# Left-over queries in plain fp32, row places and kept norms on GpSimd, and the weighting of the values spread over two slots of an attention pipeline

## The chip, the cores and the metric

The program runs on one core of one Trainium2 chip. The metric is the device time of one execution in microseconds. TensorE is called PE in the profile (PEld is its weight load), VectorE DVE, ScalarE ACT, GpSimd POOL and the DMA-issuing SyncE SP.

## The reference, cut to what matters

Each of 32 images is cut into 196 patches, projected to 128 features, joined with 77 text tokens to N = 273 tokens, and sent through attention with mixed heads and then through a mixture of 8 experts with two chosen per token. All is fp32.

```python
h = concatenate([tok(x), txt], axis=1)                  # 32 x 273 x 128
qkv = layernorm(h) @ w_qkv.T + b_qkv                    # 8 heads of 16
q, k = rope2d(q), rope2d(k)
logits = einsum('bhid,bhjd->bhij', q, k) * d ** -0.5
logits = einsum('bhij,gh->bgij', logits, w_pre)         # heads mixed before ...
attn = softmax(logits)
attn = einsum('bhij,gh->bgij', attn, w_post)            # ... and after the softmax
h = h + einsum('bhij,bhjd->bhid', attn, v) @ w_out.T + b_out
y = layernorm(h)
top_p, top_i = top_k(softmax(layer_norm(y, ln_g, ln_b) @ Wg), 2)     # two experts per token
h = h + layer_norm(y + combined, out_g, out_b)          # combined: two experts' outputs by their shares
```

## The kernel before, in words

**The two halves.** A first stage runs over the images (32 steps and two more to drain) and does tokens, attention, and the routing of each image's rows into a DRAM table `routed`. A second stage runs the experts over 76 tiles of 256 routed rows, and a third adds the results up. The change is in the first stage, but for two waits behind it.

**The first stage.** The head mix `w_pre` is folded into the queries (a head's query is the whole 128-feature query times a column of factors), and the mix `w_post` into the values (`VP`, one copy of the values for each head). So a head's scores are one product of 128 features with 273 keys. 273 queries are two tiles of 128 (`MQ` = 256) and `RT` = 17 left-over ones; the left-over queries of all 8 heads are packed into two tiles of 68 rows. One step `i` is thus 9 slots `u` (`NU`): slot 0 scores the left-over queries (`qrf`, split into `qrh` and `qrl`), slots 1 to 8 one head each. Each engine has an order of its own, written out by hand in its `step(i, par, has)`, and they meet only in semaphores. `par` is the parity of the step, which chooses between double buffers. The step is a software pipeline over four images: in step `i` image `i` is in attention, image `i + 1` is embedded (`emb`), image `i - 1` gets its residual (`res`), image `i - 2` is routed (`rout`), and the rows of image `i - 3` are scattered (`late`). Steps 4 to 29 are a hardware loop of two steps a turn, the others are written out.

**Per slot.** PE multiplies scores (`scores`, L1258, into two PSUM banks), transposes the probabilities of three slots earlier (`probs_T`), and multiplies those of four slots earlier with `VP` (`weighted`). DVE takes the sums' reciprocals and scales half of the probabilities of the slot before (`row_sums`, `head_probs`), takes the row maxima (`head_max`), and makes the low part of a query tile (`q_lo`). ACT copies the transposed probabilities to SBUF (`probsT`, L709), scales the other half (`scaled`), makes the high part of a query tile (`q_hi`) and takes the exponentials (`exps`, L682). POOL scales the left-over queries' part (`rest_keys`, L503). A scores product of fp32 precision is three fp32r products: high by high, high by low, low by high.

**What stands where around the change.** Slot 1 and 2 of PE: `x2T_` (L1335, the transposes of image `i - 2`, which need `xhat` of ACT, L762), then `tok` (L1225, 12 matmuls each, the tokens of image `i + 1`), which write the PSUM bank `MA` that the values of image `i` lie in, and so wait until `values` of DVE (L916 twice, and L922 into `VR`) has read them. `values` is called in DVE's slot 0. Slot 8 of PE: `rank` (the places of the rows within each expert, L1354 to L1358) and then `vproj` (L1255, the values of image `i + 1`, into `MA`). Slot 8 of DVE: `k_lo` (L939), `qr_lo` (L934), `q_lo`, and `places` (L1020 to L1032): position of each row from `rank` and the running `base`, times the two choice masks `mk`, summed over the 8 experts, cast to integers `slu`. POOL's `scatter` (L564, six indirect DMAs) uses `slu` in slots 0 and 1 of the next step. POOL's slot 5 has `norm2` (L513 to L525, powers on 98x3), its slot 6 `rope_add` of the queries (L486, `qT`) and `rest_queries` (L494, `qrf`), its slot 7 `rope_add` of the keys (`kT`) and the routing masks. ACT has `qr_hi` (L666) in slot 7 and `k_hi` (L745) in slot 8. DVE's `keep` (L982) copies the norms of image `i - 2` into `kept`, read at the end of the program. After the last image DVE makes the tile table from `base` (L1113 to L1140) and SP writes the tails and loads tiles.

Of the kernel before, what the change touches and what calls it, by code (L numbers as in the profile page):

```python
# [25 lines left out]
B, C, IMG, P16 = 32, 3, 224, 16  # L26
HP = IMG // P16
TXT, D, NH, DH = 77, 128, 8, 16
NE, FH = 8, 512
# [3 lines left out]
NT = 3  # L33
# [51 lines left out]
def early_fusion_kernel(nc, x, txt, w_tok, w_qkvr, small_in, w1, b2, w2, rope, tail, tiota,  # L85
# [5 lines left out]
    with ctx:  # L91
# [22 lines left out]
        rounded_ = sb("rounded", [D, 4 * NP + 8 * MQ + 2 * NH * RT], f32r)  # L114
# [41 lines left out]
        at += 2 * QR * MQ  # L156
        qrh, qrl = (rounded_[:, at + i * NH * RT:at + (i + 1) * NH * RT] for i in range(2))
# [44 lines left out]
        slf = sb("slf", [R, 2, NT])  # L202
# [25 lines left out]
        def parts(buf, count, size, at=0):  # L228
# [21 lines left out]
            k_hi k_lo q_hi q_lo qr qr_hi qr_lo vp scores_ps max exp recip probs probs_act own probsT_ps probsT_sb av_ps attn_sb proj_ps h1  # L250
            rstd2 rstd2_steps y2 xhat x2T_ps x2T_sb gate_ps gate_sb top8 logit_gap gap_exp choice_steps masks both
            share_steps routed_cols rank_ps pos_steps pos_read slots scat0 scat1 table_steps table_ready ends_ready
# [175 lines left out]
        def _(pool):  # L428
# [45 lines left out]
            def rope_add(b, par, n):  # L474
# [6 lines left out]
                else:  # L481
                    if not below(b, 1):
                        pool.wait_ge(S["k_hi"], b)
                        pool.wait_ge(S["k_lo"], b)
                    dst = kT[:]
                g_.tensor_tensor(dst, rc[:, n, :], rsn[:, n, :], ALU.add).then_inc(S["qk_sb"], 1)  # L486

            def rest_queries(b, par):

                pool.wait_ge(S["qk_sb"], 2 * b + 1)  # L490
                if not below(b, 1):
                    pool.wait_ge(S["qr_hi"], b)
                    pool.wait_ge(S["qr_lo"], b)
# [12 lines left out]
            def norm2(b):  # L506
# [18 lines left out]
                g_.tensor_tensor(rr2[:], tv2[:, 0], mhalf[:], ALU.pow).then_inc(st, 1)  # L525

# [28 lines left out]

            def scatter(j, par, k):
# [45 lines left out]
            steps(pool, step)  # L602
            scatter(B - 1, 1, 0)
# [37 lines left out]
        def _(act):  # L641
# [19 lines left out]

            def qr_hi(b):
                act.wait_ge(S["qr"], b + 1)
                if not below(b, 1):
                    act.wait_ge(S["scores_ps"], NU * (b - 1) + 1)
                nc.scalar.copy(qrh[:], qrf[:].rearrange("p g n -> p (g n)")).then_inc(S["qr_hi"], 1)  # L666
# [100 lines left out]
            qr_hi(0)  # L767
# [3 lines left out]
            def step(i, par, has):  # L771
                for u in range(NU):
# [26 lines left out]
                    if u == 7 and has["emb"]:  # L799
                        qr_hi(i + 1)  # L800
# [48 lines left out]
        def _(dve):  # L849
# [82 lines left out]
            def qr_lo(b):  # L932
                dve.wait_ge(S["qr_hi"], b + 1)
                v.tensor_tensor(qrl[:], qrf[:].rearrange("p g n -> p (g n)"), qrh[:].bitcast(f32), ALU.subtract  # L934
                                ).then_inc(S["qr_lo"], 1)

# [42 lines left out]
            def keep(j):  # L979

                dve.wait_ge(S["rstd2"], j + 1)
                v.tensor_copy(kept[:, bass.ds(j, 1)].rearrange("p a n t -> p (a n) t"), nr2[:])  # L982

# [18 lines left out]
            def experts(j):  # L1002
# [12 lines left out]
            def places(j, par):  # L1015

                st = S["pos_steps"]
# [535 lines left out]
```

## Time and profile before

| | us |
|---|---|
| Three runs | 1542.67, 1545.71, 1545.99 (median 1545.71) |
| The profiled execution, its own time | 1548.41 |
| Its span in the trace | 1546.6 |
| Busy: PE, PEld, DVE, ACT, POOL | 1213.4, 1094.2, 1102.9, 1049.4, 885.5 |
| Image step, from the starts of the 32 copies of L731 | 32.8 |

The profiled execution has 1.8 us around its span, and stands 0.17% above the median. The first image step's slots begin at about 29 us, the last attention step ends near 1083 us, and experts and sums fill the rest. All busy shares are averages over these stages. The granted PE clock is 0.931 over the whole span and 1.00 in the steps quoted below.

### The profile page before, as it was taken

To read this page: it belongs to the slowest core of one execution; us is meant where nothing else is said; L and a number is where in the kernel's file an instruction comes from. 1 tells how busy PE (TensorE), PEld (TensorE's weight loads), DVE (VectorE), ACT (ScalarE), POOL (GpSimd) and SP (SyncE) were. 2 spreads that over 40 slices of the span, in tenths; PEclk is the share of its full clock that TensorE was granted. 3 is DMA by queue.
4 is the path that set the end of the run, shared out by engine and by line. 5 is a ranking of instruction groups with operands and counts; after the bars stand their busy time and mean duration, and the time that the engine had idled before them with its cause. 6 is when DMAs were issued, how large, how long until landed. Compare 5 with 4: busy or idle time off the path is not lost.

```text
span 1546.6 us, 36424 instructions
## 1 busy us (share of the span) xinstructions
PE 1213.4 (78%) x8770; PEld 1094.2 (71%) x8771; DVE 1102.9 (71%) x3668; ACT 1049.4 (68%) x3071; POOL 885.5 (57%) x1653
## 2 busy tenths in 40 slices
PE   5898888888888888888888888888459999996000
PEld 4777777777777777777777777777359999996000
DVE  4877887788877888877888878886145445443887
ACT  2688777777777877777777777777035555553665
POOL 2136555556555556554565555565436666675998
PEclk8999999999999999999999999999579999998555
DMA  5001110010111010110010110100032222222454
GB/s 219 18 26 30 47 37 30 29 33 29 46 34 32 29 33 29 47 35 30 29 33 29 49 34 29 33 14 16 18 88 78 79 74 76 77 75 65 140 156 133
DMA packets 69517, 82.80 MB, mean 54 GB/s; under 512 B 11626, under 2 KB 59725, under 8 KB 68898
## 3 DMA queue, kind: packets, MB, share of 16 engines
q1 hardware_dynamic: 57216, 57.16, 12.6%
q0 software_dynamic: 11328, 19.07, 4.1%
q10 hardware_dynamic: 866, 5.55, 0.9%
q14 instruction: 89, 0.73, 0.2%
q8 instruction: 18, 0.29, 0.1%
HBM read 52.08 MB, written 30.65 MB: 53 GB/s over the span
## 4 chain that ended last, share of the span: by engine, by line
PE 40%; DVE 25%; issue 15%; POOL 8%; ACT 7%; DVEq 2%; DMA 1%; SPq 1%; ACTq 0%; POOLq 0%
PE PS L1464 9%; PE PS L1225 6%; PE PS L1311 4%; DVE rounded L929 4%; DVE nmax L965 4%; ACT E L682 3%; PE PS L1451 2%; PE PS L1452 2%; PE PS L1453 2%; DVE VP L916 2%; PE PS L1248 2%; DVE bst L871 2%; DVE sl L1024 2%; POOL rs L634 2%; DVE xn L896 2%
## 5 line engine op out<-in xcount | busy, mean ns | idle before, releaser
L1311 PE MATMUL PS<-AT,VP 128*128 128x273 f32 x1024 | 281.3, 397 | 0.0
L682 ACT ACTIVATE E<-PS,nmax 128x273 f32<-128x273 f32 x512 | 243.6, 482 | 36.5 <-DVE nmax L965 36.3
L965 DVE TENSOR_REDUCE nmax<-PS 128x2 f32<-128x546 f32 (+1 forms) x288 | 205.9, 715 | 73.5 <-PE PS L1273 73.5
L564 POOL DMA_INDIRECT dram_routed<-xr,slu x192 | 203.7, 1061 | 64.5 <-issue 64.5
L1271 PE MATMUL PS<-rounded 128*128 128x274 f32 (+1 forms) x576 | 209.1, 363 | 5.0 <-DVE rounded L934 3.1
L615 POOL DMA_INDIRECT dram_results<-arena,du x152 | 166.1, 1093 | 64.2 <-issue 54.6
L1311 PEld LDWEIGHTS PS<-AT,VP 128*128 128x128 f32 x1024 | 177.0, 193 | 21.0
L1291 PE MATMUL PS<-small,E 128*128 128x128 f32 x1024 | 157.6, 276 | 39.8 <-ACT ATR L716 39.8
L1272 PE MATMUL PS<-rounded 128*128 128x274 f32 (+1 forms) x576 | 169.4, 294 | 0.0
L1273 PE MATMUL PS<-rounded 128*128 128x274 f32 (+1 forms) x576 | 168.9, 293 | 0.0
L709 ACT COPY AT<-PS 128x512 f32<-128x512 f32 x256 | 151.3, 591 | 24.2 <-PE PS L1291 19.9
L503 POOL TENSOR_TENSOR EK<-E,rsum 128x34 f32<-128x34 f32 x256 | 71.6, 280 | 148.5 <-DVE rsum L944 147.7
L1464 PE MATMUL PS<-w2s,VP 128*128 x1216 | 156.4, 278 | 0.1
L1291 PEld LDWEIGHTS PS<-small,E 128*128 128x128 f32 x1024 | 122.2, 141 | 47.0 <-ACT ATR L716 46.6
L695 ACT ACTIVATE E<-E,rsum 128x256 f32<-128x256 f32 x256 | 131.8, 515 | 26.4 <-DVE rsum L944 24.3
L1464 PEld LDWEIGHTS PS<-w2s,VP 128*128 128x128 f32 x1216 | 148.4, 192 | 0.3 <-issue 0.3
L950 DVE TENSOR_SCALAR E<-E,rsum 128x256 f32<-128x256 f32 x256 | 141.9, 554 | 9.0
L659 ACT ACTIVATE rounded<-qT,small 128x256 fp32r<-128x256 f32 x256 | 128.2, 502 | 25.6 <-POOL qT L486 25.6
L821 ACT ACTIVATE VP<-PS,b1f 128x256 f32<-128x256 f32 x304 | 119.3, 475 | 29.4 <-PE PS L1453 29.4
L1225 PE MATMUL PS<-wtok,arena 128*98 128x128 f32 x768 | 101.2, 284 | 26.2 <-DVE VR L922 17.3
L929 DVE SCALAR_TENSOR_TENSOR rounded<-qT,small,rounded 128x256 fp32r<-128x256 f32 x256 | 121.7, 475 | 0.0
L1271 PEld LDWEIGHTS PS<-rounded 128*128 128x128 f32 (+1 forms) x576 | 108.0, 188 | 12.0 <-DVE rounded L934 3.4
(194 smaller groups left out, 3144.7 us busy)
## 6 DMA issues: line engine op xcount, KB each, us to landing
arena<-in_x SPq DMA_DIRECT2D x32, 588.0 KB, 3.8
arena<-dram_routed SPq DMA_DIRECT2D x76, 144.0 KB, 2.2
stage<-dram_results SPq DMA_DIRECT2D x32, 196.0 KB
dram_h<-H SPq DMA_DIRECT2D x32, 147.0 KB
w1hl<-dram_h SPq DMA_DIRECT2D x32, 147.0 KB
out<-w1hl SPq DMA_DIRECT2D x32, 98.0 KB
dram_routed<-xr,slu POOLq DMA_INDIRECT x192, 2.3
stage<-dram_results SPq DMA_DIRECT2D x32, 77.0 KB
```

The source lines that it names most:

```text
L564: g_.indirect_dma_start(out=routed, out_offset=bass.IndirectOffsetOnAxis(ap=slu[0:rows, par, k, t:t + 1], axis=0), in_=xr[0:rows, par, t, ...
L615: g_.indirect_dma_start(out=results.rearrange("n (k d) -> (n k) d", k=2), out_offset=bass.IndirectOffsetOnAxis(ap=du[:, u, h, :], axis=0), ...
L682: nc.scalar.activation(bank, PS[0:rows, 2 * ((par + u) % 2) + t, 0:N], ACT.Exp, bias=nmax[0:rows, u, t:t + 1], accum_out=esum[0:rows, u, t ...
L929: v.scalar_tensor_tensor(qlo[:, g % QR, :], qT[:, par, 0:MQ], wpre[:, g:g + 1], qhi[:, g % QR, :].bitcast(f32), ALU.mult, ALU.subtract).th ...
L965: v.tensor_reduce(nmax[0:rows, u], PS[0:rows, b0:b0 + 2, 0:N], AX.X, ALU.max, negate=True).then_inc(S["max"], 1)
L1225: last = mm(PS[0:R, MA, t * D:(t + 1) * D], xt[:, p, q, t * R:(t + 1) * R], wtok[:, q, :], start=(q == 0), stop=(q == QP - 1))
L1271: mm(o, hi, khi[:, par, 0:NV], start=True, stop=False)
L1272: mm(o, hi, klo[:, par, 0:NV], start=False, stop=False)
L1273: last = mm(o, lo, khi[:, par, 0:NV], start=False, stop=True)
L1291: last = tr(PS[:, TB, at:at + 128], E[:, (u - 1) % EB, t, keys], idn[:])
L1311: last = mm(acc, VP[:, par, g, c, :], AT[:, g, c, :], start=(g == 0 and c == 0), stop=False)
L1464: mm(o, GT[:, u % 2, c, h * 128:(h + 1) * 128], w2s[:, bass.ds(e * FH + c * D, D)], start=(c == 0), stop=False)
```

## The change

The left-over queries are scored as one plain fp32 product each (`qrf` by `kT`) in place of three fp32r products; `qr_hi`, `qr_lo` and their buffers go, and the waits on `qr_lo` and `k_lo` in slot 0 become waits on `qr` and `qk_sb`. DVE's `places` keeps the position and the base; the masks' product, the sum over 8 experts (three halving additions) and the cast move to POOL as `place`, called in slot 0 of the next step ahead of `scatter`. `keep` moves to the end of POOL's `norm2`. PE's `vproj` moves up in slot 8, behind `probs_T`, and the first half of `values` moves from DVE's slot 0 to its slot 8, ahead of `places`.

```diff
@@ gpsimd, rope_add and rest_queries
                         pool.wait_ge(S["k_lo"], b)
+                        pool.wait_ge(S["scores_ps"], NU * (b - 1) + 1)
...
-                    pool.wait_ge(S["qr_hi"], b)
-                    pool.wait_ge(S["qr_lo"], b)
+                    pool.wait_ge(S["scores_ps"], NU * (b - 1) + 1)
@@ gpsimd, end of norm2
+                pool.wait_ge(S["rstd2"], b + 1)
+                g_.tensor_tensor(kept[:, bass.ds(b, 1)].rearrange("p a n t -> p (a n) t"), nr2[:],
+                                 one3[:].unsqueeze(1).broadcast_to([R, 2, NT]), ALU.mult).then_inc(S["kept_norm"], 1)
@@ gpsimd, new
+            def place(j, par):
+
+                st = S["pos_steps"]
+                pool.wait_ge(S["pos"], j + 1)
+                g_.tensor_tensor(sl[:], mk[:], ps_[:].unsqueeze(1).broadcast_to([R, 2, NT, NE]), ALU.mult
+                                 ).then_inc(st, 1)
+                pool.wait_ge(st, 4 * j + 1)
+                for n, half in enumerate((4, 2, 1)):
+                    g_.tensor_tensor(sl[:, :, :, 0:half], sl[:, :, :, 0:half], sl[:, :, :, half:2 * half], ALU.add
+                                     ).then_inc(st, 1)
+                    pool.wait_ge(st, 4 * j + 2 + n)
+                if not below(j, 2):
+                    pool.wait_ge(S[f"scat{par}"], 48 * (j - par))
+                carry_wait(par)
+                g_.tensor_copy(slu[:, par], sl[:, :, :, 0]).then_inc(S["slots"], 1)
@@ gpsimd, step and after it
+                    if u == 0 and has["late"]:
+                        place(i - 3, 1 - par)
                     if u == (0 if has["res"] else 7) and has["late"]:
                         scatter(i - 3, 1 - par, 0)
...
+            place(B - 1, 1)
             scatter(B - 1, 1, 0)
@@ scalar: qr_hi and its calls go
-                    if u == 7 and has["emb"]:
-                        qr_hi(i + 1)
@@ vector: qr_lo and keep and their calls go
@@ vector, experts
+                if not below(j, 1):
+                    dve.wait_ge(S["slots"], j)
                 v.tensor_tensor(mk[:], eq[:], cst[:, 0:2], ALU.mult).then_inc(S["masks"], 1)
@@ vector, places
                 dve.wait_ge(S["rank_ps"], j + 1)
-                dve.wait_ge(S["routed_cols"], j + 1)
+                if not below(j, 1):
+                    dve.wait_ge(S["slots"], j)
+                    dve.wait_ge(S["pos_read"], j)
                 v.tensor_tensor(ps_[:], PS[0:R, MB, 0:NT * NE].rearrange("p (t e) -> p t e", t=NT),
-                                base[:].unsqueeze(1).broadcast_to([R, NT, NE]), ALU.add).then_inc(st, 1)
-                dve.wait_ge(st, 3 * j + 1)
-                for k in range(2):
-                    v.tensor_tensor(sl[:, k], mk[:, k], ps_[:], ALU.mult)
+                                base[:].unsqueeze(1).broadcast_to([R, NT, NE]), ALU.add).then_inc(S["pos"], 1)
+                dve.wait_ge(S["pos"], j + 1)
                 v.tensor_tensor(base[:], PS[0:R, MB, NT * NE:(NT + 1) * NE], base[:], ALU.add
                                 ).then_inc(S["pos_read"], 1)
-                dve.wait_ge(S["pos_read"], j + 1)
-                v.tensor_reduce(slf[:], sl[:], AX.X, ALU.add).then_inc(st, 1)
-                dve.wait_ge(st, 3 * j + 2)
-                v.tensor_copy(slu[:, par], slf[:]).then_inc(st, 1)
-                dve.wait_ge(st, 3 * j + 3)
-                v.tensor_copy(hold[:, 2:3], slf[:, 0, 0:1]).then_inc(S["slots"], 1)
@@ vector, step (behind q_lo)
+                    if u == 8 and has["emb"]:
+                        values(i + 1, 1 - par, 0)
                     if u == 0 and has["attn"] and has["res"]:
-                        for half in range(2):
-                            values(i, par, half)
+                        values(i, par, 1)
@@ vector, after the steps
+            dve.wait_ge(S["pos_read"], B)
             dve.wait_ge(S["w2_loaded"], 48)
@@ tensor, scores
                 if u == 0:
-                    pe.wait_ge(S["qr_lo"], i + 1)
-                    pe.wait_ge(S["k_lo"], i + 1)
+                    pe.wait_ge(S["qr"], i + 1)
+                    pe.wait_ge(S["qk_sb"], 2 * i + 2)
                 else:
                     pe.wait_ge(S["q_lo"], NH * i + u)
+                    if u == 1:
+                        pe.wait_ge(S["k_lo"], i + 1)
...
+                    if u == 0:
+                        last = mm(PS[0:RM, bank + t, 0:N], qrf[:].rearrange("p g n -> p (g n)")[:, t * RM:(t + 1) * RM],
+                                  kT[:, 0:N], start=True, stop=True)
@@ tensor, step
                     if head:
                         probs_T(*head)
+                    if u == 8 and emb:
+                        vproj(i + 1)
...
                     if u == 8 and has["rout"]:
                         rank(i - 2, emb)
-                    if u == 8 and emb:
-                        vproj(i + 1)
```

## Rows read from the trace of the kernel before

**Rows 1.** The page's chain that ended last, by line; it covers the whole span.

```profile
PE PS L1464 9%; PE PS L1225 6%; PE PS L1311 4%; DVE rounded L929 4%; DVE nmax L965 4%; ACT E L682 3%; PE PS L1451 2%; PE PS L1452 2%; PE PS L1453 2%; DVE VP L916 2%; PE PS L1248 2%; DVE bst L871 2%; DVE sl L1024 2%; POOL rs L634 2%; DVE xn L896 2%
```

**Rows 2.** Line 731, once an image: count, ns min/median/max, first and last start.

```profile
L731 ACT COPY xnT<-PS x32: 411/422/424, 19.1 to 1035.6; 128x294 f32<-128x294 f32 x32
```

**Rows 3.** The waits: engine, line, releaser: us in total, times, longest us.

```profile
PE PS L1335 <- ACT xr L762: 25.5, 30, 1.4
...
PE PS L1225 <- DVE VR L922: 17.3, 30, 1.0
```

**Rows 4.** Timeline of PE: start us, us, engine, line, [idle before it, releaser].

```profile
519.10 0.62 PE L1317 MATMUL PS<-ATR,VR 68*128 68x273 f32 x2
519.56 0.18 PE L1354 MATMUL PS<-msb,trb 98*98 98x24 bf16 x1
...
519.82 0.69 PE L1255 MATMUL PS<-wqkv,xnT 128*128 128x128 f32 x4
...
520.48 0.37 PE L1271 MATMUL PS<-rounded 128*68 128x274 f32 x1
...
521.31 0.60 PE L1291 MATMUL PS<-small,E 128*128 128x128 f32 x4
...
525.50 0.47 PE L1335 MATMUL PS<-small,xr 98*128 98x98 f32 x3 [0.55 <-ACT xr L762]
526.63 1.52 PE L1225 MATMUL PS<-wtok,arena 128*98 128x128 f32 x12 [0.65 <-DVE VR L922]
```

**Rows 5.** Timeline of DVE, same stretch and columns.

```profile
519.36 0.50 DVE L939 TENSOR_TENSOR rounded<-kT,rounded 128x294 fp32r<-128x294 f32 x1 [0.32 <-ACT rounded L745]
519.78 0.33 DVE L934 TENSOR_TENSOR rounded<-qrf,rounded 128x136 fp32r<-128x136 f32 x1
...
520.43 0.17 DVE L1020 TENSOR_TENSOR pos<-PS,base 98x24 f32<-98x24 f32 x1
...
522.23 0.17 DVE L944 RECIPROCAL rsum<-esum 128x2 f32<-128x2 f32 x1
...
523.81 2.34 DVE L916 TENSOR_TENSOR VP<-PS,small 128x1024 f32<-128x1024 f32 x2
526.08 0.41 DVE L922 TENSOR_TENSOR VR<-PS,small 68x256 f32<-68x256 f32 x1
...
534.66 0.73 DVE L965 TENSOR_REDUCE nmax<-PS 128x2 f32<-128x546 f32 x1 [2.28 <-PE PS L1273]
```

**Rows 6.** Timeline of ACT, same stretch and columns.

```profile
517.52 0.31 ACT L666 CAST rounded<-qrf 128x136 fp32r<-128x136 f32 x1
517.73 1.27 ACT L752 ACTIVATE y<-H,nr 98x128 f32<-98x128 f32 x3
...
523.53 0.49 ACT L682 ACTIVATE ER<-PS,nmax 68x273 f32<-68x273 f32 x1 [0.19 <-DVE nmax L965]
...
524.47 0.98 ACT L762 ACTIVATE xr<-y,rr 98x128 f32<-98x128 f32 x3
```

**Rows 7.** Timeline of POOL, same stretch and columns.

```profile
522.47 0.24 POOL L503 TENSOR_TENSOR EK<-E,rsum 128x34 f32<-128x34 f32 x1 [1.03 <-DVE rsum L944]
...
537.39 0.19 POOL L460 TENSOR_TENSOR rs<-mv,epsT 98x3 f32<-98x3 f32 x1 [5.15 <-DVE mv L876]
```

**Rows 8.** Timeline, DVE and POOL in slot 7, same columns.

```profile
546.73 1.46 DVE L950 TENSOR_SCALAR E<-E,rsum 128x256 f32<-128x256 f32 x1
...
547.23 0.81 POOL L486 TENSOR_TENSOR qT<-rc,rsn 128x294 f32<-128x294 f32 x1
```

**Rows 9.** Line 950: count, ns min/median/max, first and last start.

```profile
L950 DVE TENSOR_SCALAR E<-E,rsum x207: 352/437/1464, 200.2 to 1047.8; 128x256 f32<-128x256 f32 x104
```

**Rows 10.** POOL's L543 by form: busy us, mean ns, idle us before.

```profile
L543 POOL TENSOR_TENSOR cm<-mk,cf 98x48 f32<-98x48 f32 x32 | 8.6, 269 | 2.5
```

**Rows 11.** Timeline of DVE after the last image, same columns as rows 4.

```profile
1119.30 0.18 DVE L1020 TENSOR_TENSOR pos<-PS,base 98x24 f32<-98x24 f32 x1 [10.54 <-POOL tokb L554]
...
1120.51 0.15 DVE L1113 CAST basu<-base 1x8 uint32<-1x8 f32 x1
```

More of the change, by code:

```diff
@@ L155, in early_fusion_kernel @@
                     for i in range(2))
-        at += 2 * QR * MQ
-        qrh, qrl = (rounded_[:, at + i * NH * RT:at + (i + 1) * NH * RT] for i in range(2))
         qrf = sb("qrf", [D, NH, RT])
@@ L249, in early_fusion_kernel @@
             tok_ps xnT_ps qk_ps v_ps h0 bn1 bn2 bn3 stats1 stats2 stats3 rstd1 rstd1_steps xn xnT_sb hb rope qk_sb
-            k_hi k_lo q_hi q_lo qr qr_hi qr_lo vp scores_ps max exp recip probs probs_act own probsT_ps probsT_sb av_ps attn_sb proj_ps h1
-            rstd2 rstd2_steps y2 xhat x2T_ps x2T_sb gate_ps gate_sb top8 logit_gap gap_exp choice_steps masks both
-            share_steps routed_cols rank_ps pos_steps pos_read slots scat0 scat1 table_steps table_ready ends_ready
+            k_hi k_lo q_hi q_lo qr vp scores_ps max exp recip probs probs_act own probsT_ps probsT_sb av_ps attn_sb proj_ps h1
+            rstd2 kept_norm rstd2_steps y2 xhat x2T_ps x2T_sb gate_ps gate_sb top8 logit_gap gap_exp choice_steps masks both
+            share_steps routed_cols rank_ps pos pos_steps pos_read slots scat0 scat1 table_steps table_ready ends_ready
             tails row0 row1 row2 row3 xT_ps w_sb x_hi x_lo hidden_ps gelu out_ps out_sb cols place out0
@@ L660, in q_hi @@
                                      ).then_inc(S["q_hi"], 1)
[L662 to L666, printed above, removed]
             def exps(i, par, u):
@@ L930, in q_lo @@
                                        qhi[:, g % QR, :].bitcast(f32), ALU.mult, ALU.subtract).then_inc(S["q_lo"], 1)
[L932 to L935, printed above, removed]
             def k_lo(b, par):
@@ L1040, in _ @@
             k_lo(0, 0)
-            qr_lo(0)
             dve.wait_ge(S["bv_ps"], 1)
@@ L1069, in step @@
                             k_lo(i + 1, 1 - par)
-                            qr_lo(i + 1)
                     lead = ahead_of(i, u, 2, has)
@@ L1088, in step @@
                     if has["rout"]:
-                        if u == 1:
-                            keep(i - 2)
                         if u == 3:
@@ L1097, in step @@
                         if u == 8:
-                            places(i - 2, par)
+                            places(i - 2)
             steps(dve, step)
@@ L1174, in stats_back @@
             def stats_back(k, p):
+                if below(k, 1):
+                    dve.wait_ge(S["kept_norm"], B)
                 if not below(k, UP):
@@ L1259, in scores @@
                 if u == 0:
-                    pe.wait_ge(S["qr_lo"], i + 1)
-                    pe.wait_ge(S["k_lo"], i + 1)
+                    pe.wait_ge(S["qr"], i + 1)
+                    pe.wait_ge(S["qk_sb"], 2 * i + 2)
                 else:
                     pe.wait_ge(S["q_lo"], NH * i + u)
+                    if u == 1:
+                        pe.wait_ge(S["k_lo"], i + 1)
                 if not (below(i, 1) and u < 2):
                     pe.wait_ge(S["exp"], 2 * (NU * i + u - 1))
+                bank = 2 * ((par + u) % 2)
                 for t in range(2):
-                    rows, cols = (RM, slice(t * RM, (t + 1) * RM)) if u == 0 else (128, slice(t * 128, (t + 1) * 128))
-                    hi, lo = (qrh[:, cols], qrl[:, cols]) if u == 0 else (qhi[:, (u - 1) % QR, cols],
-                                                                          qlo[:, (u - 1) % QR, cols])
-                    o = PS[0:rows, 2 * ((par + u) % 2) + t, 0:NV]
-                    mm(o, hi, khi[:, par, 0:NV], start=True, stop=False)
-                    mm(o, hi, klo[:, par, 0:NV], start=False, stop=False)
-                    last = mm(o, lo, khi[:, par, 0:NV], start=False, stop=True)
+                    if u == 0:
+                        last = mm(PS[0:RM, bank + t, 0:N], qrf[:].rearrange("p g n -> p (g n)")[:, t * RM:(t + 1) * RM],
+                                  kT[:, 0:N], start=True, stop=True)
+                    else:
+                        hi, lo = (q[:, (u - 1) % QR, t * 128:(t + 1) * 128] for q in (qhi, qlo))
+                        o = PS[:, bank + t, 0:NV]
+                        mm(o, hi, khi[:, par, 0:NV], start=True, stop=False)
+                        mm(o, hi, klo[:, par, 0:NV], start=False, stop=False)
+                        last = mm(o, lo, khi[:, par, 0:NV], start=False, stop=True)
                 last.then_inc(S["scores_ps"], 1)
```

10 lines of the change are left out of this document (2 added, 8 removed).

## The prediction

> **What bounds the kernel now.** I read the page's chain first: the experts' matmuls (L1464) lead it, and behind them stand lines of the image steps on three engines, none above 6% [rows 1]. So no engine alone bounds the image steps; they are a loop of waits. Its period: the 32 copies of L731 start from 19.1 to 1035.6, so (1035.6 - 19.1) / 31 = 32.8 us per image [rows 2]. What is saved in a step counts 30 times or so, and only if it lies on that loop.
>
> The waits then say where PE stands still in it: 25.5 us in 30 times until `xr` of ACT is there (0.85 each) and right behind it 17.3 us in 30 times until DVE has written `VR` (0.58 each) [rows 3]. The timelines of one step show the knot. PE ends slot 1's `weighted`, waits 0.55 for `xr`, transposes, waits 0.65 for `VR` and starts `tok` at 526.63 [rows 4]. From there PE has no idle time until it has made the scores of slot 3; DVE then stands idle 2.28 us until 534.66 for these scores [rows 5]. That idle time tells that nothing but PE's row of work from `tok` on sets the rest of the step: whatever makes `tok` start earlier moves the whole step. Before `tok`, in slots 8 and 0, it is DVE that is late: `k_lo` 519.36, `qr_lo` 519.78, `places` from 520.43 until the next reciprocal at 522.23, the two halves of `VP` from 523.81 to 526.08, then `VR` of 0.41 [rows 5].
>
> **DVE, slots 8 and 0.** From `qr_lo`'s start to `pos` are 0.65 us, which hold `qr_lo` and `q_lo`; by its own row `qr_lo` is 0.33, of which some 0.25 is in the order (starts overlap ends by 0.08). `places` takes 522.23 - 520.43 = 1.80; kept are the position (0.17) and the base with a wait between, together some 0.45, so 1.35 goes. The first half of `VP` comes in: (526.08 - 523.81) / 2 = 1.13. `k_lo` itself begins 517.73 - 517.52 = 0.21 earlier, as ACT drops `qr_hi` ahead of it [rows 6]. The reciprocal of slot 0 thus moves by 0.21 + 0.25 + 1.35 - 1.13 = 0.68 to 521.55. `VR` gains the half of `VP` as well: 0.68 + 1.13 = 1.81, to be written at 526.49 - 1.81 = 524.7. `values` in slot 8 needs `vproj`, which moves from 519.82 to behind the transposes, ahead of the four matmuls of `weighted` that end where L1317 starts (519.10 less 4 x 0.23, about 518.2); it takes 0.66 [rows 4], and is there before DVE asks at 520.0. Without the move DVE would wait for it; with it `weighted` and `rank` come 0.66 later, and only `pos` at 521.1 asks for `rank`, done by 520.6.
>
> **PE, slot 0.** The three-product scores of the left-over queries take 521.31 - 520.48 = 0.83. The plain fp32 products are priced by L1317: the same 273 columns, 68 rows, two of them from 519.10, and the next matmul starts at 519.56, so 0.46 [rows 4]. So 0.37 goes. Their old wait for `qr_lo` (520.11) ended just before PE came, so its end gives nothing.
>
> The Trainium skill speaks against this part: "FP8 and Floating Point Precision", section TensorE Precision Notes, has true fp32 as four passes through the array. Priced by the fp32r products here (0.83 / 6 = 0.14 each) two products would be 8 x 0.14 = 1.1 us, slower than the 0.83 that go. The row of L1317 has under half of that, and I go by the row.
>
> **ACT, slot 0.** What PE waits for first is `xr` (524.47 and 0.98 long), which stands behind the exponentials of slot 0 (523.53) [rows 6]. These wait for DVE's maxima, 0.68 earlier, but ACT first copies PE's transposes, 0.37 earlier, scales and makes a query tile. The advance of `xr` lies between 0.21 (only `qr_hi` gone) and 0.68; I take 0.5, nearer to what holds it now (DVE's maxima, by the bracket of that row).
>
> **What `tok` gains.** The wait for `VR` ends: `VR` is there at 524.7, the transposes of `xr` end at 525.45 by the above. So `tok` follows them at once: 0.58 (the mean wait) plus 0.5 is 1.08 us per image, between 0.79 and 1.26. What is late next is `xr`, and PE's own row behind it.
>
> **POOL, slot 0.** `place` comes ahead of the six scatters. Its product is of the form of L543 (98x48, 269 ns), the three additions lie between 0.19 (98x3, L460 [rows 7]) and 0.27, each with 0.08 idle by its own wait (2.5 us in 32) [rows 10], then the hold and the cast: 0.35 + 3 x 0.31 + 0.4 = 1.7 us; at the dearest elementwise row here, 0.81 each [rows 8], it would be 4.9. Queued behind it are the scatters and `rest_keys` of slots 1 and 2. POOL stands idle for 5.15 us until 537.39 for DVE's statistics [rows 7], which come 1.1 earlier now: cover of 4.0 us for the 1.7. Beyond it each us would be paid in full. `experts` waits for `slots` five slots later: nothing.
>
> **POOL, slot 5 and 6.** `kept_norm` adds one instruction of the size of L460, 0.19 [rows 7], ahead of `rest_keys` and the queries' rope. This is not covered. DVE's scaling (L950) in slot 7 starts at 546.73 and ends only at 548.19, just behind POOL's rope addition, which ends at 548.04 [rows 8]; its median is 0.44 and its least 0.35 [rows 9]. So DVE, and ACT's next query tile, stand behind POOL here, and the addition goes through: +0.2 per image, at most 0.3 with a register computation for the address, at least 0 were it hidden. `keep` going from DVE saves nothing: behind it DVE waits for ACT.
>
> The Trainium skill has a name for the row: "SBUF — State Buffer", section "SBUF: two separate sides", says that DVE and GpSimd lock a shared port for a whole instruction and the loser blocks. The trace agrees in the 1.46 us; the rule would also let DVE win wherever it starts first, which is one of the rivals below.
>
> **The end.** `places` no longer waits for POOL's routing columns (the last one waited 10.54 us for them, at 1119.30), and the base is ready for the table without the sums that now fill most of 1120.51 - 1119.30 = 1.21 [rows 11]. The same happens an image earlier. Against that the last scatters start behind `place`. Between 0 and 2.5; I take 1.
>
> **The sum.** 1.08 - 0.2 = 0.88 per image, times 30 steps = 26.4, plus 1 = 27.4 us. From the profiled execution's 1548.41 (span 1546.6) that gives 1521.0; the median of the runs stands 2.7 lower, so the forecast is 1545.7 - 27.4 = 1518. With both ends of the unknown terms: (0.79 - 0.3) x 30 = 14.7 and (1.26 - 0) x 30 + 2.5 = 40, that is 1531 and 1506.
>
> **Rivals.**
> 1. *`xr` doesn't move.* POOL's `place` and `rest_keys` run just as DVE scales slot 8's probabilities; if DVE is held there by some 0.5 us (`rest_keys` 0.24 [rows 7] and the product 0.27), the maxima, the exponentials and `xr` come when they come now. Then only the wait for `VR` is gained: (0.58 - 0.2) x 30 + 1 = 12.4, so 1533. For it: the 1.46 us of slot 7. Against it: `rest_keys` is there today, and `place` has pauses of 0.08 between its instructions.
> 2. *DVE slips in.* If POOL pauses at `kept_norm` (an address from a register) for long enough, DVE's scaling in slot 7 starts in the pause and its 1.1 us of standing go. Gain 27.4 + 0.9 x 30 = 54, so 1491. Against it: POOL's instructions there stand end to start, and waits already met made no pause.
> 3. *Slower.* DVE is held in slot 0 behind all of `place`, as it is in slot 7 behind a row of POOL's instructions. L950 would end at about 523.9 in place of 522.1, 1.8 later, and `xr`, and so `tok`, 0.5 after today's 526.63; with the 0.2, 0.7 x 30 = 21 us more: 1567. It decides from a hold of 1.3 us on. For it: the same mechanism is in the trace. Against it: the pauses, and that at least half of all L950 in the step, slot 8's among them, take no more than 0.44 now.
> 4. *Nothing measurable*: `tok` is earlier, but in slots 3 to 8 an order of ACT and POOL that I hold for shifted as a whole is not. The idle 2.28 us of DVE speak against it.
> 5. *Plain products are dear.* They take 1.1 and not 0.46 us. ACT's copy of the transposes behind them and `xr` come 0.27 later than now: (0.58 - 0.27 - 0.2) x 30 + 1 = 4.3, so 1541. The row of L1317, with the same columns, rows and type, speaks against it.
>
> **How the numbers follow.** The forecast has 0.59, rival 1 0.19, rival 2 0.06, rival 3 0.08, rival 4 0.06, rival 5 0.02. What a measurement of this kernel can tell from no change is about 0.2%, 3 us. Faster by more: 0.59 + 0.19 + 0.06 + 0.02 = 0.86; slower: 0.08; the same: 0.06. The range runs from 1506 to 1534: it holds the forecast with its bounds and rival 1, and leaves out the others.
>
> **What would show it.** PE's wait for `VR` gone from the waits, that for `xr` still there; `tok` 1.1 us earlier behind ACT's `ATR` copy of slot 7; L731's copies 31.9 us apart in place of 32.8; two plain products 0.23 us apart in slot 0; `place` 1.5 to 2 us and POOL's idle time before L460 down to some 2.5 us; L950 of slot 7 at 1.46 or up to 0.2 above. I am wrong if `tok` is early and the period is not, or if L950 of slot 8 is above 0.8.

## The result, and the profile after

| | before | after |
|---|---|---|
| Median of 4 runs each | 1544.19 (1539.27 to 1545.99) | 1505.44 (1505.30 to 1506.03) |
| Ratio, 95% interval | | 0.975 (0.9729 to 0.977) |
| The profiled execution, its own time | 1548.41 | 1505.31 |
| Its span | 1546.6 | 1503.5 |
| First expert tile starts at | 1135.2 | 1091.9 |

The kernel is 38.8 us faster; 27.4 were forecast, and the time lies just under the range. All times here are of fast runs: one execution of `a_three_pad64` (experiment 13) took 1880 us at a granted clock of 0.64, and is left out of its median. The rows of after that answer to those of before come first. The page's chain, by line [rows 1]:

```profile
PE PS L1464 9%; PE PS L1220 6%; PE PS L1311 5%; PE PS L1451 3%; PE PS L1291 2%; PE PS L1452 2%; PE PS L1453 2%; POOL rs L653 2%; DVE bst L881 2%; ACT E L695 2%; DVE rounded L939 2%; POOL w1hl L644 2%; ACT ER L695 2%; POOL qT L484 2%; POOL nr L512 2%
```

DVE's maxima, its `VP` and `sl` have left it, and POOL's `norm2` (L512) and rope addition (L484) are in it. The copies of `xnT` [rows 2], and the waits [rows 3; us in total, times, longest]:

```profile
L744 ACT COPY xnT<-PS x32: 410/422/424, 17.8 to 998.3; 128x294 f32<-128x294 f32 x32
```

```profile
ACT rounded L678 <- POOL qT L484: 33.4, 30, 1.3
...
ACT AT L722 <- PE PS L1311: 18.0, 12, 1.7
...
PE PS L1335 <- ACT xr L775: 15.8, 30, 0.9
```

(998.3 - 17.8) / 31 = 31.6 us per image in place of 32.8. The wait for `VR` is gone, as said; that for `xr` fell from 25.5 to 15.8. New among ScalarE's long waits is the middle row: 12 waits of 1.5 us, and 12 is the number of times that the loop over pairs of images goes back to its start (13 passes). I call that jump back "the turn". PE in slots 8 and 0 [rows 4], and DVE beside it [rows 5]:

```profile
561.34 0.62 PE L1317 MATMUL PS<-ATR,VR 68*128 68x273 f32 x2
...
562.06 1.12 PE L1266 MATMUL PS<-kT,qrf 128*68 128x273 f32 x4
563.01 0.60 PE L1291 MATMUL PS<-small,E 128*128 128x128 f32 x4
...
566.90 0.47 PE L1335 MATMUL PS<-small,xr 98*128 98x98 f32 x3 [0.24 <-ACT xr L775]
567.22 1.51 PE L1220 MATMUL PS<-wtok,arena 128*98 128x128 f32 x12
```

```profile
560.93 0.55 DVE L944 TENSOR_TENSOR rounded<-kT,rounded 128x294 fp32r<-128x294 f32 x1 [0.74 <-ACT rounded L758]
561.40 0.47 DVE L939 SCALAR_TENSOR_TENSOR rounded<-qT,small,rounded 128x256 fp32r<-128x256 f32 x1
561.80 1.21 DVE L926 TENSOR_TENSOR VP<-PS,small 128x1024 f32<-128x1024 f32 x1
...
563.24 0.17 DVE L949 RECIPROCAL rsum<-esum 128x2 f32<-128x2 f32 x1
...
565.96 0.41 DVE L932 TENSOR_TENSOR VR<-PS,small 68x256 f32<-68x256 f32 x1
```

L1266 is the two plain products: 563.01 - 562.06 = 0.95 us, where the six fp32r products took 0.83 and 0.46 was forecast. Its row has x4 records for two products. So L1317's x2, from which I took the price, was one product: `weighted_rest` issues only one.

Medians over the steps of the loop, from one start to the next (left of the slash the steps without the turn, right of it those with it):

| us | before | after | forecast |
|---|---|---|---|
| `norm2` to the `ATR` copy of slot 7 | 6.12 / 6.12 | 5.93 / 5.82 | +0.2 |
| `ATR` copy to `xr` | 7.22 / 7.78 | 7.04 / 7.99 | -0.5 |
| `xr` to its transposes | 1.03 / 1.11 | 1.03 / 1.11 | 0 |
| transposes to `tok` | 1.13 / 0.92 | 0.31 / 0.32 | -0.58 |
| `tok` to the next `norm2` | 17.13 / 17.16 | 17.11 / 17.16 | 0 |
| period | 32.63 / 33.08 | 31.44 / 32.43 | -0.88 |

The net is -0.93 an image. That it is close to the forecast's -0.88 is luck: the first term is some 0.45 below its forecast, the second some 0.5 above, and the two cancel. The 43.1 us between the two profiled executions are: 31 x 0.93 = 28.8 in the periods, 4.7 in three periods of before that are some 34.6 long in place of 33.1, 2.5 in the first periods, 1.3 before the first `xnT`, 6.0 from the last `xnT` to the first expert tile, and 0.2 given back behind it.

### The profile page after: what moved, and what is told of

The parts are those of the page before. It is cut to its first block, busy times and chain, and to the rows that moved or that the text cites. A ratio compares the mean times of both kernels' runs of the same rounds, so it can differ in the third digit from the quotient of the medians.

```text
span 1503.5 us, 36457 instructions
## 1 busy us (share of the span) xinstructions
PE 1204.4 (80%) x8706; PEld 1076.4 (72%) x8707; DVE 1020.0 (68%) x3444; ACT 1035.3 (69%) x3039; POOL 933.6 (62%) x1877
## 4 chain that ended last, share of the span: by engine, by line
PE 43%; POOL 18%; issue 18%; DVE 10%; ACT 8%; DMA 1%; POOLq 1%; DVEq 1%; ACTq 1%; SPq 0%
PE PS L1464 9%; PE PS L1220 6%; PE PS L1311 5%; PE PS L1451 3%; PE PS L1291 2%; PE PS L1452 2%; PE PS L1453 2%; POOL rs L653 2%; DVE bst L881 2%; ACT E L695 2%; DVE rounded L939 2%; POOL w1hl L644 2%; ACT ER L695 2%; POOL qT L484 2%; POOL nr L512 2%
## 5 line engine op out<-in xcount | busy, mean ns | idle before, releaser
L1311 PE MATMUL PS<-AT,VP 128*128 128x273 f32 x1024 | 278.9, 394 | 0.0
L580 POOL DMA_INDIRECT dram_routed<-xr,slu x192 | 189.2, 986 | 62.3 <-issue 61.7
L1311 PEld LDWEIGHTS PS<-AT,VP 128*128 128x128 f32 x1024 | 175.5, 191 | 20.6
L1271 PE MATMUL PS<-rounded 128*128 128x274 f32 x512 | 186.1, 364 | 3.7 <-ACT E L695 2.1
L1272 PE MATMUL PS<-rounded 128*128 128x274 f32 x512 | 149.0, 291 | 0.0
L1273 PE MATMUL PS<-rounded 128*128 128x274 f32 x512 | 148.8, 291 | 0.0
L949 DVE RECIPROCAL rsum<-esum 128x2 f32<-128x2 f32 (+1 forms) x288 | 45.1, 157 | 135.0 <-ACT E L695 127.6
L500 POOL TENSOR_TENSOR EK<-E,rsum 128x34 f32<-128x34 f32 x256 | 67.8, 271 | 95.2 <-DVE rsum L949 94.1
L955 DVE TENSOR_SCALAR E<-E,rsum 128x256 f32<-128x256 f32 x256 | 107.5, 420 | 9.0
L822 ACT CAST rounded<-PS 128x256 fp32r<-128x256 f32 x76 | 28.4, 373 | 123.4 <-PE PS L1439 123.4
```

The costliest lines, as they stand in the source:

```text
L580: g_.indirect_dma_start(out=routed, out_offset=bass.IndirectOffsetOnAxis(ap=slu[0:rows, par, k, t:t + 1], axis=0), in_=xr[0:rows, par, t, ...
L1271: mm(o, hi, khi[:, par, 0:NV], start=True, stop=False)
L1272: mm(o, hi, klo[:, par, 0:NV], start=False, stop=False)
L1273: last = mm(o, lo, khi[:, par, 0:NV], start=False, stop=True)
L1311: last = mm(acc, VP[:, par, g, c, :], AT[:, g, c, :], start=(g == 0 and c == 0), stop=False)
```

## The experiments

Each kernel was timed in five rounds beside the kernel before, 4 to 12 executions each; the times are medians, the ratios (with 95% intervals) are to that kernel. The runs stem from four batches, in which the kernel before had medians from 1543.3 to 1545.5. So a difference between runs of two batches is good to some 2 us, and a saving by medians can differ by as much from the one by ratios. Names with `a_` start from the changed kernel (1505.4), names with `b_` from the one before.

**1. `a_pad64`: where ScalarE's loop lies.**

```diff
+            for k in range(64):
+                nc.scalar.copy(pad[:, 1 + k:2 + k], pad[:, 0:1])
             def q_hi(i, par, g):
```

> The changed kernel with 64 one-element copies put ahead of ScalarE's first work, while it waits for the weights; nothing else differs. In the changed kernel's trace ScalarE's first record of a new turn of the image loop comes 3.0 us after the branch record, VectorE's and GpSimd's 0.3 after theirs, and instruction-fetch packets run in that time. Theory 1 (the fetch at the turn, and where the loop lies among the instructions decides it): the 3.0 falls under 0.6, the idle 1.47 us ahead of the AT copy falls to some 0.55, and 12 turns x 0.9 = 11 us go: 1494. Rival: the copy waits for PE's weighted products, as the wait's releaser says; nothing moves: 1505.

Measured: 1494.83, 0.9689 (0.9672 to 0.9705), theory 1: 10.6 us for copies that compute nothing. (VectorE sets the tile that they read, and ScalarE waits for it once.) The records of the loop's own line at one turn in the changed kernel (ACTq is ScalarE's sequencer; the last numbers are first and last start):

```profile
L293 ACTq COMPARE_BRANCH  x1: 45/45/45, 592.7 to 592.7; - x1
...
L293 DVEq COMPARE_BRANCH  x1: 56/56/56, 594.5 to 594.5; - x1
L293 DVEq FUSED_REGOPS  x1: 85/85/85, 594.8 to 594.8; - x1
...
L293 ACTq FUSED_REGOPS  x1: 59/59/59, 595.7 to 595.7; - x1
```

and the copy that comes next on ScalarE:

```profile
595.89 0.59 ACT L722 COPY AT<-PS 128x512 f32<-128x512 f32 x1 [1.46 <-PE PS L1311]
```

The same line in the padded kernel:

```profile
L294 ACTq COMPARE_BRANCH  x1: 45/45/45, 588.0 to 588.0; - x1
...
L294 ACTq FUSED_REGOPS  x1: 59/59/59, 588.2 to 588.2; - x1
```

3.0 us became 0.2. The DMA view between 200 and 990 us (packets, MB) counts the packets that carry instructions, first of the changed kernel, then of the padded one:

```profile
q14 instruction: 62, 0.51, 0.2%
```

```profile
q14 instruction: 3, 0.02, 0.0%
```

So the wait's releaser (L1311) was wrong: ScalarE was fetching its own instructions. Of the five packets of 8 KB a turn two lie within the 3.0 us and take 0.9 of them; how the rest of the 3.0 is spent, no view shows. The turn's period fell from 32.4 to 31.57, the other stayed at 31.43. The Trainium skill has this in "Runtime: NRT & Kernel Launch", section Instruction fetch mechanics: a taken branch to a target outside the fetched pages waits for a DMA. The packets agree. Only a shift of 64 instructions was tried.

**2. `a_three`: the left-over queries in three fp32r products again.**

```diff
-                        last = mm(..., qrf[...], kT[:, 0:N], start=True, stop=True)
+                    mm(o, hi, khi[:, par, 0:NV], start=True, stop=False)
+                    mm(o, hi, klo[:, par, 0:NV], start=False, stop=False)
+                    last = mm(o, lo, khi[:, par, 0:NV], start=False, stop=True)
```

> The changed kernel with the left-over queries scored in three fp32r products again (qr_hi on ScalarE, qr_lo on VectorE back). Theory 1 (two plain products take 0.95 us, not 0.46): PE's slot 0 becomes 0.12 us shorter, VectorE 0.25 and ScalarE 0.21 longer, of which ScalarE's lies under the wait for POOL's kT: 1503 to 1511. Rival (the forecast's price, 0.46): PE 0.37 longer and qr_lo 0.25 more ahead of the maxima, 0.4 to 0.6 an image: 1517 to 1523.

Measured: 1502.37, 0.9736 (0.9722 to 0.9749), just under theory 1's range; the forecast's price is out. The plain products cost some 3 us in this kernel (3.1 by the medians, 2.2 by the ratios). `ATR` to `xr` is 6.90 with three products and 7.04 with plain ones.

**3. `a_place_dve`: the places on VectorE again** (`place` goes, `places` has its sum, cast and hold back).

> The changed kernel with the places computed on VectorE again; kept norms stay on GpSimd. VectorE gets 1.35 us in slot 8. Theory 1: after the change VectorE's maxima of slot 0 are ready 1.0 us before ScalarE takes them in the loop's turn, so 0.35 to 0.8 an image is paid: 1516 to 1530. Rival (the forecast's row, in which VectorE is what the step waits for): all 1.35 an image: 1545. Second rival: VectorE's slack covers it: 1505.

Measured: 1521.39, 0.9861 (0.9846 to 0.9876): +16.0, theory 1. `ATR` to `xr` grows by 0.62 / 0.22. From the last `xnT` copy to the first expert tile it has 96.4 us, the changed kernel 93.6: 2.8 of the end are this part's.

**4. `a_keep_dve`: the kept norms on VectorE again.**

```diff
-                g_.tensor_tensor(kept[:, bass.ds(b, 1)]..., nr2[:], one3[:]..., ALU.mult)
+                v.tensor_copy(kept[:, bass.ds(j, 1)]..., nr2[:])
```

> The changed kernel with the kept norms copied by VectorE in slot 1 again. Theory 1 (GpSimd's row from norm2 to qT and kT bounds slots 5 to 8, kept_norm's 0.2 goes through it): 0.2 x 30 = 6 us go: 1499.5. Rival (kept_norm is what opened the port for VectorE's scaling in slot 7, 0.95 and 0.35 in place of 1.46): that goes back to 1.46 in both halves, 0.5 to 1.1 an image: 1518 to 1532. Second rival: nothing, 1505.

Measured: 1511.38, 0.9797 (0.9784 to 0.981): +6.0. My theory has the wrong sign and the rival's mechanism is there, though at less than half its price. VectorE's scaling, all slots (ns min/median/max), in this kernel and in the changed one:

```profile
L952 DVE TENSOR_SCALAR E<-E,rsum x196: 352/435/1461, 202.5 to 984.5; 128x256 f32<-128x256 f32 x196
```

```profile
L955 DVE TENSOR_SCALAR E<-E,rsum x198: 352/355/959, 201.1 to 987.4; 128x256 f32<-128x256 f32 x198
```

The 1.46 of [rows 8, 9] is back, and `norm2` to `ATR` is 6.11 again.

**5. `a_kept_fixed`: the same product on GpSimd into a fixed tile, the norms kept by VectorE.**

```diff
+                g_.tensor_tensor(spare[:], nr2[:], one3[:]..., ALU.mult)
```

> The changed kernel with the kept norms copied by VectorE again and, in kept_norm's place on GpSimd, the same product into a fixed tile (no address from a register). Theory 1 (the pause before kept_norm for its address let VectorE's scaling in): the scaling of slot 7 goes back to 1.46, and the product's 0.2 is paid besides: 1511 to 1518. Rival (any short instruction there shifts the two engines enough): as the changed kernel, 1503 to 1508.

Measured: 1503.38, 0.9746 (0.9729 to 0.9763). The rival: it is not the address.

```profile
L955 DVE TENSOR_SCALAR E<-E,rsum x198: 352/372/857, 202.2 to 988.3; 128x256 f32<-128x256 f32 x198
```

A short instruction more on GpSimd between `rr` and `EK` is enough to shorten the scaling of slot 7, here to 0.85 us.

**6. `b_place_keep`: the kernel before with only places and kept norms on GpSimd.**

> The kernel before with only the places and the kept norms on GpSimd. Theory 1: VectorE 1.35 us shorter in slot 8 and VectorE's scaling of slot 7 slips in between GpSimd's instructions (0.18 an image, by the opposite experiment): the wait for VR goes (0.58), xr some 0.3 earlier: 1.06 x 30 = 32 us, 1511. Rival (places was hidden): 0.2 an image or less, 1537 and above.

Measured: 1510.01, 0.9786 (0.9765 to 0.9807): -35.5 (-33 by the ratio) of the whole change's 38.8. Theory 1.

**7. `b_vp`: the kernel before with only the divided weighting and the earlier projection** (`vproj` moves on PE as in the change).

```diff
+                    if u == 8 and has["emb"]:
+                        values(i + 1, 1 - par, 0)
                     if u == 0 and has["attn"] and has["res"]:
-                        for half in range(2):
-                            values(i, par, half)
+                        values(i, par, 1)
```

> The kernel before with only the divided weighting and the earlier projection. Theory 1: VectorE gets 1.13 us more in slot 8, where ScalarE waits for its maxima, VR is not earlier; xr comes 1.13 later and the wait of 0.58 for VR goes: 0.55 x 30 = 16 us more, 1560. Rival (dividing spreads VectorE's load and helps by itself): 1530 or less. Second rival: nothing, 1543.

Measured: 1528.43, 0.9901 (0.988 to 0.9921): -17 (-15 by the ratio), where I expected +16; the rival's number, though the cause proved another. `xr` came 0.48 later, not 1.13, and `VR` 0.66 earlier, not at its time. So 0.66 us of work vanished from VectorE. The kernel before, VectorE and GpSimd in slot 8:

```profile
520.58 0.86 POOL L471 TENSOR_TENSOR HB<-H,small 98x384 f32<-98x384 f32 x1
...
520.63 0.94 DVE L1024 TENSOR_TENSOR sl<-mk,pos 98x24 f32<-98x24 f32 x2
```

The two small products begin 0.05 us behind POOL's addition and end just behind it. In `b_vp` the half of `VP` stands beside that addition, and the products come later and take 0.28:

```profile
509.50 1.21 DVE L916 TENSOR_TENSOR VP<-PS,small 128x1024 f32<-128x1024 f32 x1
...
509.64 0.87 POOL L471 TENSOR_TENSOR HB<-H,small 98x384 f32<-98x384 f32 x1
...
510.84 0.28 DVE L1024 TENSOR_TENSOR sl<-mk,pos 98x24 f32<-98x24 f32 x2
```

**8. `b_hb`: that addition moved.**

```diff
-                    if u == 8 and has["emb"]:
-                        hb(i + 1, 1 - par)
+                    if u == 1 and has["attn"] and has["res"]:
+                        hb(i, par)
```

> The kernel before with GpSimd's HB addition moved from slot 8 to slot 1, behind the scatters; nothing else. Theory 1 (VectorE's products for the places stand 0.66 us behind that addition: 0.94 beside it, 0.28 in the kernel with the divided weighting, where they run at another time): the products fall to 0.3, VR is written 0.66 earlier, xr 0.3 to 0.66: 15 to 20 us, 1524 to 1530. Rival (the 0.94 is the products' own time, or the addition stops something else in slot 1): 1540 and above.

Measured: 1522.63, 0.9863 (0.9845 to 0.9881): -20.6 for one instruction at another place. Line 1024 of the kernel before, and of this one:

```profile
L1024 DVE TENSOR_TENSOR sl<-mk,pos x38: 169/506/846, 420.3 to 1014.0; 98x24 f32<-98x24 f32 x38
```

```profile
L1024 DVE TENSOR_TENSOR sl<-mk,pos x38: 175/180/184, 442.3 to 1021.5; 98x24 f32<-98x24 f32 x38
```

`VR` is written 0.65 earlier (`ATR` to `VR` 8.83 to 8.18), `xr` 0.30 / 0.67, and the period falls by 0.67 / 0.67 (to 31.96 / 32.41). Theory 1, shown. The Trainium skill, "SBUF — State Buffer", section "SBUF: two separate sides", names among what can be held a VectorE operation with two operands in SBUF, against a GpSimd one that reads SBUF. The two products have both operands there; the weighting reads PSUM, and its half takes 1.21 beside the addition (experiment 7, slot 8) and 1.21 without it. The rows agree.

**9. `b_vproj`: only the earlier projection.**

> The kernel before with only PE's projection of the values moved ahead of weighted; the weighting stays in slot 0. Theory 1 (the 16 us of the divided weighting came from VectorE's order alone): 1541 to 1547. Rival (they came from PE's order): 1528 to 1532.

Measured: 1551.76, 1.0044 (1.0029 to 1.0059). Neither. The periods are those of before (32.60 / 33.1), so PE's order gave nothing; but six periods are 34.6 long in its profile, three in that of before. The three more, at 1.6 each, are 4.8 of the 6.8 us by which this kernel is slower. In such a period PE's granted clock fell to half. Windows of before around one (columns: the window and its length, busy us and instructions of PE, PEld, DVE, ACT, POOL, the granted clock, DMA share and GB/s):

```profile
289.00:291.00 2.00, 2.00 (x15) 1.84 (x15) 1.69 (x5) 1.44 (x4) 1.00 (x3) 1.00 0.47 83
291.00:293.00 2.00, 0.82 (x6) 0.40 (x4) 2.00 (x2) 2.00 (x8) 1.70 (x2) 1.00 0.69 270
293.00:295.00 2.00, 1.55 (x14) 1.39 (x13) 1.71 (x6) 1.46 (x5) 1.39 (x3) 0.93 0.11 28
295.00:297.00 2.00, 2.00 (x11) 2.00 (x10) 0.56 (x3) 1.40 (x5) 1.69 (x2) 0.50 0.17 51
```

PE stood 1.18 us in the second window, for `xr`, and 0.45 in the third, for `VR`; then the clock is at 0.5 (1.2 GHz) for some 3.4 us, which costs the period 1.6.

**10. `a_vp_back`: the divided weighting and the projection undone.**

> The changed kernel with both halves of the values' weighting in slot 0 and the projection behind the ranks again. Theory 1 (VectorE's work up to VR is the same sum either way, and VR is written 1.3 us or more before tok could use it): VR not later, the maxima of slot 0 up to 1.1 earlier but not waited for: 1503 to 1507. Rival (this part is what the run gained above the other parts, because tok waits for VR again): 0.5 an image, 1520 and above.

Measured: 1512.75, 0.9795 (0.9775 to 0.9814): +7.3; theory 1 fell. `VR` comes 1.07 / 0.66 later, so the sum on VectorE is not the same either way. Without the turn `tok` waits for it again (transposes to `tok` 0.62 in place of 0.31): the rival's mechanism, at less than its price. VectorE's row ahead of slot 0:

```profile
568.21 0.17 DVE L949 RECIPROCAL rsum<-esum 128x2 f32<-128x2 f32 x1 [0.99 <-ACT E L695]
```

Without `places` VectorE stands 0.99 us idle at the end of slot 8 for ScalarE's exponentials; the half of `VP` fills that.

**11. `b_plain`: the kernel before with only the plain products.**

> The kernel before with only the plain fp32 scores of the left-over queries. Theory 1 (0.95 us for the two products): PE 0.12 longer, which ScalarE's copy of the transposes meets, VectorE 0.25 shorter: between 0.25 less and 0.12 more an image, 1536 to 1547. Rival (the forecast's 0.46): 0.4 an image or more, 1531 or less.

Measured: 1538.5, 0.9961 (0.9948 to 0.9974): 6 us by the ratio, in theory 1's range. But its periods are those of before (32.64 / 33.10), so VectorE's 0.25 gave nothing there. What it gains is outside them: its profile has no period of 34.6, and its first period, from the first `xnT` copy to the second, is 27.8 us in place of 29.3. That goes with this part: in the nine profiles with plain products the first period is 27.1 to 27.8, in the nine with three 28.6 to 29.5.

**12. `b_pad64`: the kernel before, padded.**

> The kernel before with the 64 one-element copies ahead of ScalarE's first work. Theory 1 (the shift takes the fetch out of the turn here too, where ScalarE's gap is 0.5 us): the turn's period of 33.1 comes down towards the other's 32.6, 12 x 0.35 = 4 us: 1539 to 1541. Rival (before had enough work queued to hide its turn): 1545.

Measured: 1544.49, 1.0 (0.9988 to 1.0012). The rival. Branch to first record fell from 2.5 to 0.23 us, and the turn's period stayed 33.1: here the branch came 2.2 us before ScalarE's queued work ended. In the changed kernel it comes 1.7 us before.

**13. `a_three_pad64`: three products, padded.**

> The changed kernel with three fp32r products for the left-over queries and the 64 copies: against the padded changed kernel (1494.8) it prices the plain products with the turn out of the way. Theory 1: in the periods without a turn three products gave 31.28 against 31.44, so 0.16 x 30 = 5 us: 1490. Rival (the 3 us of the unpadded pair came from the turn alone): 1495.

Measured: 1498.93, 0.9711 (0.9692 to 0.973). Both wrong: 4.1 *above* the padded kernel with plain products (3.4 by the ratios). Periods 31.28 / 31.96 against 31.43 / 31.57. Plain products cost 0.15 in a step without the turn and give 0.39 in the one with it. My reading, which no run tests: VectorE, 0.34 us idle at its own turn, is late there and has `qr_lo` to do besides. So the sign of what they are worth depends on what else is late.

**14 to 16. GpSimd's order.** `a_order_pad64` moves the second half of `norm2` with `kept_norm` behind `rest_queries` and `shares` behind the keys' rope; `a_norm_pad64` moves only the first; `a_order_three_pad64` is the former with three products.

```diff
                             rest_queries(i + 1, 1 - par)
+                        if has["res"]:
+                            norm2_rest(i - 1)
-                        if has["rout"]:
-                            shares(i - 2)
...
                             rope_add(i + 1, 1 - par, 1)
                         if has["rout"]:
+                            shares(i - 2)
                             both_masks(i - 2)
```

> The padded changed kernel with GpSimd's order changed in slots 5 to 7: the second half of norm2 and kept_norm (1.6 us) behind the queries' rope and rest_queries, the shares (1.3) behind the keys' rope. Theory 1 (GpSimd's row from the statistics to qT and kT bounds these slots; ScalarE waits 1.03 for qT): 0.7 to 1.0 an image: 1465 to 1474. Rival (ScalarE and PE are late by themselves there): 0.3 or less, 1486 to 1495. Second rival (VectorE's scaling in slot 7 meets GpSimd's row again): 1500.

> The padded changed kernel with only the second half of norm2 and kept_norm behind rest_queries; the shares stay ahead of the keys' rope. Theory 1 (what the new order gave, 0.2 an image, came from qT alone, since behind ScalarE's ATR copy PE's own row now sets the pace): 1487 to 1491. Rival (kT's part of it counts): 1492 to 1496.

> The last two together: GpSimd's new order and three fp32r products, padded. Theory 1 (the gains add): 5 us under the kernel with the new order alone. Rival (with qT and kT early, ScalarE's and VectorE's rounding of the left-over queries is what slot 8 waits for): the same as it or above.

Measured: 1489.03, 0.9651 (0.9634 to 0.9669); 1493.4, 0.9679 (0.9663 to 0.9694); 1496.67, 0.9696 (0.968 to 0.9713). Each time the rival's range. `qT` comes 1.3 us earlier (`norm2` to `qT` 3.63 to 2.32), the `ATR` copy only 0.2 to 0.35, and 0.1 in the third. ScalarE's long waits between 200 and 1000 us fit that, first in `a_pad64`, then in `a_order_pad64`: that for `qT` is gone, and that for PE's transposes has grown.

```profile
ACT rounded L683 <- POOL qT L485: 28.2, 26, 1.2
...
ACT AT L727 <- PE PS L1297: 16.6, 37, 0.6
```

```profile
ACT AT L732 <- PE PS L1302: 28.4, 38, 1.3
```

The first of the three, 55 us faster than the kernel before and 16 faster than the changed one, is the best kernel run. Its 5.8 us under `a_pad64` are only in part explained: its periods are 31.14 / 31.79 against 31.43 / 31.57, shorter without the turn and longer with it, where one scaling of VectorE takes 0.82 in place of 0.44; and the two profiled executions are 1.7 apart.

## Why the prediction was wrong

**What failed, in short.** Two steps of the prediction. First the term for all that lies outside the steady periods: "times 30 steps = 26.4, plus 1". This took the time out of the range. Those stretches gave 14.3 us between the profiled executions (43.1 less 28.8 in the periods), some 10 between the medians. Second the price of the plain products, 0.46 us for 0.95, with `xr`'s advance and `kept_norm`'s sign; in the periods these errors cancelled. With the periods as measured and that "plus 1" the time would be 1545.7 - 29.8 = 1516, inside the range. A slip besides: the upper bound of the gain, 1.26 x 30 + 2.5, is 40.3 and not 40, which is 1505.4, where the result lies.

**The waits of PE.** Right: the wait for `VR` ended (-0.71 for -0.58), and what follows `tok` did not change.

**The plain products: failed.** "two of them from 519.10 ... so 0.46" read two records as two products. It is 0.95: the premise of rival 5, given 0.02, at 0.95 instead of its 1.1, though not rival 5's 1541, as other terms moved too. By itself this error makes the kernel slower than forecast, so it doesn't explain the miss. The Trainium skill, "FP8 and Floating Point Precision", section TensorE Precision Notes, has four passes for true fp32. The runs are nearer to that than to my reading: one product takes 0.46 to 0.48, some 3.4 fp32r products of 0.14, where I had 1.7. I had also counted the four records of `weighted` as four products; the code issues two.

**`xr`.** Forecast -0.5; measured -0.18 without the turn and +0.21 with it. The plain products hold the first back by 0.14 (experiment 2); the other 0.18 of the miss stays open. The second is ScalarE's instruction fetch, which no step of mine had: with it gone (experiment 1) the turn's `ATR` to `xr` is 7.18, -0.60.

**Places.** The price of 1.35 was right as a sum of the rows, but 0.66 of it was a stall behind `HB` (experiments 7 and 8). It stood in [rows 1] as `sl L1024 2%`, for two 98x24 products. I added it up instead of asking why they took 0.94. As the divided weighting removes the same stall, the parts do not add: -35.5 and -17 alone (-33 and -15 by the ratios), -38.8 together.

**The divided weighting.** I had it as +1.13 on the maxima of slot 0. In the changed kernel it fills VectorE's idle time (experiment 10) and is worth 7.3 us.

**`kept_norm`.** Forecast +0.2 an image, measured -0.2 (experiment 4): rival 2's mechanism, in part: the scaling of slot 7 takes 0.35 in one step and 0.95 in the other, not 1.46.

**`place` on GpSimd.** Mechanism right, size short, and hidden. GpSimd in the changed kernel:

```profile
563.68 0.34 POOL L560 TENSOR_TENSOR sl<-mk,pos 98x48 f32<-98x48 f32 x1
564.10 1.48 POOL L564 TENSOR_TENSOR sl<-sl 98x24 f32<-98x24 f32 x3
...
565.88 0.19 POOL L570 CAST slu<-sl 98x6 uint32<-98x6 f32 x1
...
577.95 0.19 POOL L457 TENSOR_TENSOR rs<-mv,epsT 98x3 f32<-98x3 f32 x1 [3.42 <-DVE mv L886]
```

566.07 - 563.68 = 2.4 us for 1.7, as the three additions take 1.48; 3.42 of the cover are left, for the 2.5 forecast.

**Outside the periods: failed, and the whole of the miss.** The per-image sum was off by only 0.05, by luck as said. Of the 15.7 us between 43.1 and 27.4, that is 2.4 with the 31st period (28.8 for 26.4); the periods of 34.6 are 4.7, the first periods and the start 3.8, the end 5.0 (6.0 for 1), and 0.2 was given back. Of the first periods' share 2.2 are the first period itself, which the plain products shorten (experiment 11). Of the end `place` gives 2.8 (experiment 3); the divided weighting alone gives 3.7 (95.9 in experiment 7 for 99.6), but only 0.4 in the changed kernel (94.0 in experiment 10 for 93.6). The kernel before also has 6.8 us at half clock there and the changed one none; but `b_plain`, also with none, has 98.6, so the clock is hardly more than 1.0 of it. The median run of before stands 4.2 under its profiled one, which leaves 11.4 between the medians.

Not settled: why the clock falls in some periods. It did 3, 2 and 6 times in the profiles of before, `b_pad64` and `b_vproj`, and in none of the 15 others; but `b_plain` has before's periods and `b_hb` its order on VectorE, without a fall. Ahead of each of the 11 falls PE had stood 1.07 to 1.45 us for `xr` and then 0.44 to 0.65 for `VR`; most such pairs of waits brought none. Nor is it settled what in GpSimd's extra instruction lets the scaling in.

## What to carry to other kernels

Before a line's duration is used as its price, divide its records by the products the code issues, and compare a small operation's time with its own minimum: what is above can be a wait in disguise, and it went here when either party moved. Two parts that remove one stall don't add. In a loop, compare the period with the turn to the one without it, and look for instruction packets there. Give the stretches ahead of the loop and behind it terms of their own.

## What the runs showed of the hardware

- One plain fp32 product of 273 columns has two matmul records of 0.23 us at full clock: 0.46 to 0.48 in all; an fp32r product of 274 has one, 0.13 to 0.14 apart.
- ScalarE's loop of 291 to 295 records an image pair took 2.5 to 3.2 us (medians of 12 kernels) from the branch to the next record, with some five instruction packets a turn; 64 instructions ahead of the loop brought that to 0.23 in all six kernels in which it was tried. VectorE with 274 to 288 records took 0.29, GpSimd 0.25 to 0.28, PE 0.27, padded or not.
- Two 98x24 products of VectorE took 0.94 us beside one GpSimd addition of 0.86, and 0.28 elsewhere; a 128x1024 product that reads PSUM took 1.21 beside it and elsewhere.
- A fall of PE's granted clock to 0.5 (1.2 GHz) for 3.4 us made a period of 33.1 us 1.6 longer (experiment 9).
